# Cross-attention kernel: the query products moved ahead of the value products, and odd slots in a second PSUM bank until the first output

## The chip, the cores and the metric

The kernel runs on one core of a Trainium2 chip. The metric is the device time of one execution in microseconds. The core has a matrix engine (TensorE, PE in the profile), which writes to the eight banks of PSUM; a vector engine (VectorE, DVE), a scalar engine (ScalarE, ACT) and a general engine (GpSimd, POOL); and a sync engine (SyncE, SP) that issues nearly all transfers. The engines run their own instruction streams in program order and meet through semaphores.

## The reference

`x` is 4 x 2048 x 640, the context 4 x 77 x 1024; of its 77 tokens the last 4 are image tokens (`ip`). There are 20 heads of 32 channels.

```
q = heads(x @ W_q); k_t = heads(text @ W_k); v_t = heads(text @ W_v)
probs_t = softmax(q k_t^T * scale)
text_out = probs_t v_t
attn_scores = q k_ip^T * scale
qsem = l2norm(probs_t @ text)                    # per head, 1024 channels
sem = qsem @ l2norm(ip)^T
probs_ip = softmax(attn_scores + 0.5 * sem) * spatial_mask
ip_out = probs_ip v_ip
out = (text_out + ip_out) @ W_out + b_out + x
```

## The kernel before

A prologue of about 88 us works the context and the weights into tables: keys per group of four heads (`kbd`), and a value table `xm` that holds, for each head, the Gram matrix of the text tokens (for the length in `l2norm`), the products with the image tokens, a column of ones and the values. Numbers that need more than 16 bits or more than the fast 32-bit form go as two parts, hi and lo, so that most products are three matmuls (hi x hi, hi x lo, lo x hi).

The main loop runs over 16 tiles of 512 rows of `x`. A tile is five slots (one for each group of four heads, 128 columns of q), a slot is two pairs of 256 rows, and a pair is one step p of the loop; there are 160, ten to a tile. All five engines have a loop over p, written out by hand, and in each the order of the work inside a step is the order of the code. In step p, PE does:

- the scores of pair p (6 matmuls to `ps_S`, L1278). In even steps they wait for the slot's query (`q_lo`), in all for DVE and ACT to have read the last scores (`s_read`, `p_ready`);
- transposes of one piece of the next tile of `x` into `ps_M` (L1294), in steps 0, 1, 2, 7 and 8 of ten;
- from step 16 on a part of the output matmuls of the tile before, in the banks `ps_O` and `ps_O2` in turn (L1257), 11 to 17 of them, in all steps of ten;
- the value products U of pair p - 2 (16 matmuls to `ps_U`, L1354), which wait for the transposed probabilities (`pts_loaded`) and for DVE to have read the last U (`attn_ready`);
- half of the query products of a coming slot m (`ps_Q`, L1368): in odd steps, p = 2m - 3, the first 7 of 15 matmuls, in even steps the other 8. The first half waits for `q_lo >= m`, that is, until DVE has read slot m - 1 out of the bank. For the first slot of a tile each three matmuls wait for their piece of `x` (`xT_lo`); the fifth piece is transposed in the same even step in which its products stand.

In step p, DVE adds finished output to `x` (L1139), takes the maximum of the scores and their bias (L1153, L1160), in odd steps forms the lo part of the query (L1127, which signals `q_lo`), forms the lo part of a piece of `x` (L1127, `xT_lo`), and only then works on U of pair p - 2 (L1185 to L1224; in odd steps some ten small instructions more, to L1241). ACT copies the hi parts of query and `x` (L1001, L1007), takes the exponentials (L1038) and copies them as 16-bit numbers (L1050), POOL forms their lo parts (L1120), and SP issues their DMA transposes (L951), which U of that pair needs two steps later.

```
PASSES = ((0, 0), (0, 1), (1, 0))
Q_MMS = [(c, a, m) for c in range(CC) for a, m in PASSES]
Q_PARTS = (Q_MMS[:7], Q_MMS[7:])
XT_AT = {-10: 0, -9: 1, -8: 2, -3: 3, -2: 4}
OUT_FROM = min(OUT_AT)      # 6
```

Of the kernel before, what the change touches and what calls it, by code (L numbers as in the profile page):

```python
# [10 lines left out]
ACT = mybir.ActivationFunctionType  # L11
# [722 lines left out]
def main_loop(nc, top, g):  # L734

    P, B, S, C, T, T_ALL, CC = (g[k] for k in "P B S C T T_ALL CC".split())
# [3 lines left out]
    ps_S2, ps_U2, ps_Q, ps_M = (g[k] for k in "ps_S2 ps_U2 ps_Q ps_M".split())  # L740
    ident, wq, wo, mask_sb, inv_out, inv_eps, ip_unit = (
        g[k] for k in "ident wq wo mask_sb inv_out inv_eps ip_unit".split())
# [5 lines left out]
    STEPS = 2 * CC  # L748
    OUTS = 2 * SUB
    X_RING, XT_RING, AT_RING, P_RING, SIP_RING, PH_RING, PT_RING = NI, 8, 10, 3, 3, 2, 2  # L750
    VW_RING = IT_RING = 2
    LU = 2
    PASSES = ((0, 0), (0, 1), (1, 0))
# [3 lines left out]
    Q_MMS = [(c, a, m) for c in range(CC) for a, m in PASSES]  # L757
    Q_PARTS = (Q_MMS[:7], Q_MMS[7:])
# [18 lines left out]
    xT = [[sb(f"xT{r}_{k}", [P, TILE], F32R) for k in range(2)] for r in range(XT_RING)]  # L777
    qT = [[sb(f"qT{r}_{k}", [P, TILE], F32R) for k in range(2)] for r in range(2)]
# [28 lines left out]
    xT_ready, xT_hi, xT_lo = g["xT_ready"], sem("xT_hi_done"), sem("xT_lo_done")  # L807
    q_ready, q_hi, q_lo = sem("q_ready"), sem("q_hi_done"), sem("q_lo_done")
# [13 lines left out]
    o_bank = [g["ps_O"], g["ps_O2"]]  # L822
# [11 lines left out]
    OUT_FROM = min(OUT_AT)  # L834
# [9 lines left out]
    def pair_of(p):  # L844
        return p if 0 <= p < PAIRS else None
# [4 lines left out]
    def q_at(p):  # L850

        part = (p + 1) % 2
        m = slot_of(p + 3 - part)
        return None if m is None else (m, part)

    def x_at(p):
# [2 lines left out]
            return [(0, c) for c in range(CC)]  # L859
        return [(j, c) for at, c in XT_AT.items() for j in range(1, TILES) if STEPS * j + at == p]  # L860

    def x_bank(j, c):
        return ps_M if j else g["x_bank0"][c]

# [16 lines left out]
    with nc.Block() as block:  # L881
# [109 lines left out]
        @block.scalar  # L991
        def _(act):
            for p in range(FIRST, LAST):

                done = q_at(p - 1)
                if done is not None and done[1] == 1:
                    m = done[0]
                    act.wait_ge(q_ready, m + 1)
                    if m >= 2:
                        act.wait_ge(s_ready, 2 * (m - 1))  # L1000
                    nc.scalar.activation(qT[m % 2][0][:], ps_Q[:], ACT.Copy).then_inc(q_hi, 1)  # L1001
                for j, c in x_at(p):
                    act.wait_ge(xT_ready, CC * j + c + 1)
                    n = CC * j + c
                    if n >= XT_RING:
                        act.wait_ge(q_ready, CC * ((n - XT_RING) // CC + 1))
                    nc.scalar.activation(xT[n % XT_RING][0][:], x_bank(j, c)[:], ACT.Copy).then_inc(xT_hi, 1)  # L1007
                i = ip_at(p)
                if i is not None:
                    act.wait_ge(pip_ready, CC * (i + 1))  # L1010
                    if i >= 1:
                        act.wait_ge(*ring(ipT_loaded, i - 1))
                    else:
                        act.wait_ge(ones_set, 1)
                    for dst in (ip16[:, :, 0, 0:IPR], ip16[:, :, 1, IPR - IP_LO:2 * IPR - IP_LO]):
                        last = nc.scalar.activation(dst, pip[:], ACT.Copy)
                    last.then_inc(ip_hi, 1)
                m = slot_of(p - 6)
                if m is not None:

                    act.wait_ge(f_ready, m + 1)
                    nc.scalar.activation(f[:], f[:], ACT.Exp, scale=SCALE).then_inc(ef_ready, 1)
                m = slot_of(p - 4)
                if m is not None:

                    act.wait_ge(attn_ready, 2 * (m + 1))
                    if m >= 2:
                        act.wait_ge(*ring(aT_loaded, m - 2))
                    nc.scalar.activation(at16[m % 2][:, 0], attn[m % 2][:].rearrange("p s h d -> p s (h d)"),
                                         ACT.Copy).then_inc(at_hi, 1)  # L1030
                if pair_of(p) is not None:

                    act.wait_ge(bias_ready, p + 1)
                    if p >= P_RING:
                        act.wait_ge(n2_done, p - P_RING + 1)
                    for j in range(2):
                        for h in range(HG):
                            last = nc.scalar.activation(pr[p % P_RING][:, j, h, :], sc[:, j, h, 0:T], ACT.Exp,  # L1038
                                                        bias=bias[p % 2][:, j, h:h + 1], scale=SCALE)
                        last.then_inc(p_ready, 1)  # L1040

                    if p < PH_RING:
                        act.wait_ge(cleared, PH_RING)
                    for j in range(2):
                        act.wait_ge(p_ready, 2 * p + j + 1)
                        if p >= PH_RING:
                            act.wait_ge(*ring(pts_loaded[j], p - PH_RING))
                        hi = ph[p % PH_RING][:, j].rearrange("p h k c -> p h (k c)")
                        for col in (0, P + LO_B):
                            last = nc.scalar.activation(hi[:, :, col:col + T], pr[p % P_RING][:, j], ACT.Copy)  # L1050
                        last.then_inc(ph_ready, 1)
# [72 lines left out]
        def _(v):  # L1124
            def lo_part(dst, src, hi, hi_done, n, signal):
                v.wait_ge(hi_done, n)
                nc.vector.tensor_tensor(dst, src, hi.bitcast(F32), ALU.subtract).then_inc(signal, 1)  # L1127
# [5 lines left out]
            for p in range(FIRST, LAST):  # L1133
# [28 lines left out]
                done = q_at(p - 1)  # L1162
                if done is not None and done[1] == 1:
                    m = done[0]
                    lo_part(qT[m % 2][1][:], ps_Q[:], qT[m % 2][0][:], q_hi, m + 1, q_lo)
                for j, c in x_at(p):
                    one = xT[(CC * j + c) % XT_RING]
                    lo_part(one[1][:], x_bank(j, c)[:], one[0][:], xT_hi, CC * j + c + 1, xT_lo)
# [76 lines left out]
        def _(pe):  # L1245
# [16 lines left out]
            for p in range(FIRST, LAST):  # L1262
                if pair_of(p) is not None:
# [8 lines left out]
                    for j in range(2):  # L1272
# [4 lines left out]
                        for a, m in PASSES:  # L1277
                            last = nc.tensor.matmul(g["ps_S"][j][:, 0:GK], qT[slot % 2][a][:, q * P:(q + 1) * P],  # L1278
                                                    kbd[:, m, slot % CC, :], start=(a, m) == PASSES[0],
                                                    stop=(a, m) == PASSES[-1])  # L1280
# [17 lines left out]
                for i, half, piece in out_at(p):  # L1298

                    n = OUTS * i + half  # L1300
                    if piece == 0 and n >= 2:
                        pe.wait_ge(o_added, n - 1)
                    if half == 0:
                        for k in range(2 * piece, min(2 * piece + 2, CC)):
                            pe.wait_ge(*ring(aT_loaded, CC * i + k))
                    if half == 0 and piece == len(O_PIECES) - 1:
                        pe.wait_ge(*ring(ipT_loaded, i))
                        if i % NI == 0:
                            b = i // NI
                            pe.wait_ge(vw_loaded[b % VW_RING], 64 * (b // VW_RING + 1) + 16)  # L1310
                    last = output_matmuls(i, half, O_PIECES[piece], o_bank[half % 2])
                    if piece == len(O_PIECES) - 1:
                        last.then_inc(o_ready, 1)

                for half, part in END_AT.get(p - PAIRS, ()):

                    i = TILES - 1
# [17 lines left out]
                    last = output_matmuls(i, half, END_PARTS[part], end_bank[half])  # L1335
                    if part == 3:
                        last.then_inc(o_ready, 1)

                u = pair_of(p - LU)
                if u is not None:  # L1340

# [12 lines left out]
                                last = nc.tensor.matmul(uo[:, j, h, :], pts[u % PT_RING][0:n, j, 2 * h + tile, :],  # L1354
                                                        xm[0:n, tile, k0 * HG + h, :], start=tile == 0, stop=tile == 1)
                    last.then_inc(u_ready, 1)

                if q_at(p) is not None:

                    m, part = q_at(p)  # L1360
                    i, k = divmod(m, CC)
                    mms = Q_PARTS[part]
                    if part == 0 and m:
                        pe.wait_ge(q_lo, m)
                    for c, a, b_ in mms:
                        if k == 0 and (a, b_) == PASSES[0]:
                            pe.wait_ge(xT_lo, CC * i + c + 1)
                        last = nc.tensor.matmul(ps_Q[:], wq[a][:, c, k * P:(k + 1) * P], xT[(CC * i + c) % XT_RING][b_][:],  # L1368
                                                start=(c, a, b_) == Q_MMS[0], stop=(c, a, b_) == Q_MMS[-1])
                    if part == 1:  # L1370
                        last.then_inc(q_ready, 1)


# [21 lines left out]
```

## Time and profile before

| | |
|---|---|
| median of 3 runs | 1023.91 us (1021.89 to 1025.69) |
| profiled execution | 1022.47 us, its span 1020.6 us |
| PE, DVE, ACT, POOL busy | 95%, 80%, 68%, 64% |
| TensorE clock granted, mean | 0.988 |
| chain that ended last | PE 77%, DMA 5%, DVE 4%, ACT 2% |

The page is of one profiled execution. PE's matmuls are pipelined: a group's record overlaps the start of the next, so where one group begins and the next begins says what it costs, and where the record ends says when its result is there. The chain is followed back from the last instruction, and says where a saved microsecond would be one at the end of the kernel.

### The profile page before, as it was taken

What the parts mean: (1) busy time and instruction counts of PE and PEld (TensorE: products, weight loads), DVE (VectorE), ACT (ScalarE), POOL (GpSimd) and SP (SyncE); (2) the same over time, 40 slices, a digit from 0 to 9 for tenths busy, and PEclk for the clock granted to TensorE, in tenths of its full rate; (3) what the DMA queues carried; (4) which work ended last, traced back from release to release, by engine and by line L of the source; (5) the groups of instructions that cost most, each with busy time, mean ns of one, the idle gap of its engine ahead of it and who ended that gap; (6) DMA issues with size and microseconds to landing.
All of it is one profiled execution on the core that took longest, in us unless ns stands there. A gap on an engine that the chain in (4) does not pass through costs nothing.

```text
span 1020.6 us, 24929 instructions
## 1 busy us (share of the span) xinstructions
PE 969.2 (95%) x7684; PEld 803.6 (79%) x7684; DVE 816.6 (80%) x2409; ACT 695.6 (68%) x2332; POOL 655.2 (64%) x1906
## 2 busy tenths in 40 slices
PE   5987788999999999999999999999999999999988
PEld 5875666888878888888887888888878888888855
DVE  6685698888888887888888888878878888878872
ACT  3534887777776777767776777777667777777740
POOL 3224587776676667677766777676667767776761
PEclk9978999999999999999999999999999999999999
DMA  9936999989889998899899989998899989887973
GB/s 293 298 117 161 195 179 186 177 163 180 168 186 186 186 185 177 163 176 162 174 178 192 192 164 191 169 167 173 167 190 187 180 169 190 137 157 154 149 138 111
DMA packets 488147, 180.27 MB, mean 177 GB/s; under 512 B 449694, under 2 KB 467155, under 8 KB 488015
## 3 DMA queue, kind: packets, MB, share of 16 engines
q1 hardware_dynamic: 487983, 178.63, 86.3%
q8 instruction: 61, 1.00, 0.4%
q14 instruction: 71, 0.58, 0.2%
q10 hardware_dynamic: 32, 0.07, 0.0%
HBM read 42.34 MB, written 27.22 MB: 68 GB/s over the span
## 4 chain that ended last, share of the span: by engine, by line
PE 77%; DMA 5%; DVE 4%; ACT 2%; issue 2%; SPq 2%; POOL 1%; DVEq 0%; ACTq 0%; POOLq 0%
PE ps_O L1257 25%; PE ps_Q L1368 25%; PE ps_S L1278 12%; PE ps_U L1354 11%; DMA pts<-ph 4%; PE ps_M L1294 3%; ACT pr L1038 2%; DMA x_in<-in_x_dram 1%; SPq L951 1%; DVE pr L1199 0%; PE ps_U L1257 0%; DVE n L1211 0%; ACT ph L1050 0%; DVE bias L1160 0%; SPq L924 0%
## 5 line engine op out<-in xcount | busy, mean ns | idle before, releaser
L1038 ACT ACTIVATE pr<-ps_S,bias 128x73 f32<-128x73 f32 x1280 | 288.8, 339 | 101.3 <-DVE bias L1160 100.1
L1120 POOL TENSOR_TENSOR ph<-pr,ph 128x220 f16<-128x220 f32 (+1 forms) x640 | 274.0, 460 | 126.2 <-ACT ph L1050 126.2
L1368 PE MATMUL ps_Q<-xT,wq_hi 128*128 128x512 f32 x800 | 280.1, 415 | 5.2 <-DVE qT L1127 5.2
L1257 PE MATMUL ps_O<-wo_hi,aT 128*128 128x320 f16 x1220 | 279.2, 300 | 0.0
L1050 ACT ACTIVATE ph<-pr 128x292 f16<-128x292 f32 x640 | 241.2, 500 | 0.0
L1257 PE MATMUL ps_O<-wo_lo,aT 128*128 128x320 f16 x610 | 182.3, 299 | 0.0
L1354 PE MATMUL ps_U<-xm,pts 128*128 128x110 f16 (+1 forms) x2560 | 159.3, 212 | 14.9 <-DMA pts<-ph 13.5
L1368 PEld LDWEIGHTS ps_Q<-xT,wq_hi 128*128 128x128 f32 x800 | 146.2, 191 | 32.7 <-DVE qT L1127 6.5
L1354 PEld LDWEIGHTS ps_U<-xm,pts 128*128 128x128 f16 (+1 forms) x2560 | 144.4, 98 | 32.3 <-issue 11.8
L1278 PE MATMUL ps_S<-kbd,qT 128*128 128x308 f32 x960 | 163.0, 304 | 2.6 <-ACT pr L1038 2.1
L1278 PEld LDWEIGHTS ps_S<-kbd,qT 128*128 128x128 f32 x960 | 150.8, 188 | 18.6 <-issue 3.0
L1368 PE MATMUL ps_Q<-xT,wq_lo 128*128 128x512 f32 x400 | 159.5, 399 | 0.0
L1257 PEld LDWEIGHTS ps_O<-wo_hi,aT 128*128 128x128 f16 x1220 | 119.2, 98 | 47.8
L1153 DVE TENSOR_REDUCE smax<-ps_S 128x8 f32<-128x584 f32 x160 | 121.6, 760 | 36.3 <-PE ps_S L1278 36.0
L1211 DVE TENSOR_REDUCE n<-pr 128x8 f32<-128x584 f32 x160 | 120.8, 755 | 0.0
L1199 DVE TENSOR_TENSOR pr<-ps_U,pr 128x584 f32<-128x584 f32 x160 | 116.9, 731 | 0.1
L1185 DVE COPY nd<-ps_U 128x40 f32<-128x40 f32 x160 | 31.5, 197 | 103.0 <-PE ps_U L1354 101.8
L1077 POOL TENSOR_TENSOR yt<-y 128x16 f32<-128x16 f32 x240 | 51.5, 215 | 91.8 <-DVE y L1241 79.2
L1007 ACT ACTIVATE xT<-ps_M 128x512 fp32r<-128x512 f32 x76 | 45.8, 603 | 76.4 <-PE ps_M L1294 76.4
L1094 POOL TENSOR_TENSOR at<-attn,at 128x512 f16<-128x512 f32 x80 | 92.7, 1159 | 0.0
L1368 PEld LDWEIGHTS ps_Q<-xT,wq_lo 128*128 128x128 f32 x400 | 76.3, 191 | 14.6
L1257 PEld LDWEIGHTS ps_O<-wo_lo,aT 128*128 128x128 f16 x610 | 59.9, 98 | 18.5
(228 smaller groups left out, 1338.9 us busy)
## 6 DMA issues: line engine op xcount, KB each, us to landing
out_dram<-x_in SPq DMA_DIRECT2D x64, 320.0 KB, 2.6
x_in<-in_x_dram SPq DMA_DIRECT2D x56, 320.0 KB, 3.2
pts<-ph SPq DMA_TRANSPOSE x320, 3.4
w_k<-in_L_xattn_W_k_dram SPq DMA_DIRECT2D x5, 512.0 KB, 8.8
w_ip<-in_L_xattn_W_k_ip_dram SPq DMA_DIRECT2D x1, 2560.0 KB, 11.0
w_v<-in_L_xattn_W_v_dram SPq DMA_DIRECT2D x5, 512.0 KB, 8.3
w_ip<-in_L_xattn_W_v_ip_dram SPq DMA_DIRECT2D x1, 2560.0 KB, 10.6
x_in<-in_x_dram SPq DMA_DIRECT2D x2, 1280.0 KB, 7.2
```

The lines of the kernel that those rows point to most:

```text
L1038: last = nc.scalar.activation(pr[p % P_RING][:, j, h, :], sc[:, j, h, 0:T], ACT.Exp, bias=bias[p % 2][:, j, h:h + 1], scale=SCALE)
L1050: last = nc.scalar.activation(hi[:, :, col:col + T], pr[p % P_RING][:, j], ACT.Copy)
L1077: nc.gpsimd.tensor_tensor(yt[:], y[:], y[:], ALU.mult).then_inc(newton_step, 1)
L1094: nc.gpsimd.tensor_tensor(at16[m % 2][:, 1], attn[m % 2][:].rearrange("p s h d -> p s (h d)"), at16[m % 2][:, 0], ALU.subtract).then_inc(a ...
L1120: nc.gpsimd.tensor_tensor(lo, full[:, :, t0:t1], one[:, :, 0, t0:t1], ALU.subtract).then_inc(pl_ready, 1)
L1153: nc.vector.tensor_reduce(smax[p % 2][:], sc[:, :, :, 0:T], AX.X, ALU.max).then_inc(max_done, 1)
L1199: nc.vector.tensor_tensor(pr[u % P_RING][:], uo[:, :, :, 0:T], pr[u % P_RING][:], ALU.mult).then_inc(prod_done, 1)
L1211: nc.vector.tensor_reduce(n2[un % 2][:, subs], pr[u % P_RING][:], AX.X, ALU.add).then_inc(n2_done, 1)
L1257: last = nc.tensor.matmul(bank[:, 0:HALF], stationary, moving, start=(k, a, b_) == O_MMS[0], stop=(k, a, b_) == O_MMS[-1])
L1278: last = nc.tensor.matmul(g["ps_S"][j][:, 0:GK], qT[slot % 2][a][:, q * P:(q + 1) * P], kbd[:, m, slot % CC, :], start=(a, m) == PASSES[0] ...
L1354: last = nc.tensor.matmul(uo[:, j, h, :], pts[u % PT_RING][0:n, j, 2 * h + tile, :], xm[0:n, tile, k0 * HG + h, :], start=tile == 0, stop= ...
L1368: last = nc.tensor.matmul(ps_Q[:], wq[a][:, c, k * P:(k + 1) * P], xT[(CC * i + c) % XT_RING][b_][:], start=(c, a, b_) == Q_MMS[0], stop=( ...
```

## The change

In PE's step the query products stand ahead of the value products; they are the same matmuls. The query products of odd slots below 8 (`FREE_SLOTS = (6 + 10) // 2`) go to `ps_O` instead of `ps_Q`, and their readers on ACT and DVE read there. Their first half waits for the last slot that used the same bank: for slots 0 to 7 two slots back, and from slot 9 on the slot before, as in the kernel before. The first output matmul waits until slot 7 has been read.

```
+    FREE_SLOTS = (OUT_FROM + STEPS) // 2
+
+    def q_bank(m):
+        return o_bank[0] if m % 2 and m < FREE_SLOTS else ps_Q
+
+    def q_bank_before(m):
+        used = [n for n in range(max(m - 2, 0), m) if q_bank(n) is q_bank(m)]
+        return used[-1] if used else None
...
-                    nc.scalar.activation(qT[m % 2][0][:], ps_Q[:], ACT.Copy).then_inc(q_hi, 1)
+                    nc.scalar.activation(qT[m % 2][0][:], q_bank(m)[:], ACT.Copy).then_inc(q_hi, 1)
...
-                    lo_part(qT[m % 2][1][:], ps_Q[:], qT[m % 2][0][:], q_hi, m + 1, q_lo)
+                    lo_part(qT[m % 2][1][:], q_bank(m)[:], qT[m % 2][0][:], q_hi, m + 1, q_lo)
...
+                    if n == 0 and piece == 0:
+                        pe.wait_ge(q_lo, FREE_SLOTS)
...
+                if q_at(p) is not None:
+
+                    m, part = q_at(p)
+                    i, k = divmod(m, CC)
+                    mms = Q_PARTS[part]
+                    if part == 0 and q_bank_before(m) is not None:
+                        pe.wait_ge(q_lo, q_bank_before(m) + 1)
+                    for c, a, b_ in mms:
+                        if k == 0 and (a, b_) == PASSES[0]:
+                            pe.wait_ge(xT_lo, CC * i + c + 1)
+                        last = nc.tensor.matmul(q_bank(m)[:], wq[a][:, c, k * P:(k + 1) * P], xT[(CC * i + c) % XT_RING][b_][:],
+                                                start=(c, a, b_) == Q_MMS[0], stop=(c, a, b_) == Q_MMS[-1])
+                    if part == 1:
+                        last.then_inc(q_ready, 1)
+
                 u = pair_of(p - LU)
                 if u is not None:
...
-                if q_at(p) is not None:
-
-                    m, part = q_at(p)
-                    i, k = divmod(m, CC)
-                    mms = Q_PARTS[part]
-                    if part == 0 and m:
-                        pe.wait_ge(q_lo, m)
```

PE, the end of an odd step of the main loop and the start of the next, before:

```order
L1257 MATMUL ps_O<-vw,ipT 128x320 x2
L1354 MATMUL ps_U<-xm,pts 128x110 [waits pts_loaded0_1,attn_ready]
L1354 MATMUL ps_U<-xm,pts 128x110 x7
L1354 MATMUL ps_U<-xm,pts 128x110 [waits pts_loaded1_1]
L1354 MATMUL ps_U<-xm,pts 128x110 x7
L1368 MATMUL ps_Q<-xT_0,wq_hi 128x512 [waits q_lo_done]
L1368 MATMUL ps_Q<-xT_1,wq_hi 128x512
```

and now:

```order
L1267 MATMUL ps_O<-vw,ipT 128x320 x2
L1361 MATMUL ps_Q<-xT_0,wq_hi 128x512 [waits q_lo_done]
L1361 MATMUL ps_Q<-xT_1,wq_hi 128x512
L1361 MATMUL ps_Q<-xT_0,wq_lo 128x512
L1361 MATMUL ps_Q<-xT_0,wq_hi 128x512
L1361 MATMUL ps_Q<-xT_1,wq_hi 128x512
L1361 MATMUL ps_Q<-xT_0,wq_lo 128x512
L1361 MATMUL ps_Q<-xT_0,wq_hi 128x512
L1381 MATMUL ps_U<-xm,pts 128x110 [waits pts_loaded0_1,attn_ready]
L1381 MATMUL ps_U<-xm,pts 128x110 x7
```

The query products and their wait for the bank moved ahead of the value products; the next step's scores now follow the value products at once.

PE, the even step in which a new tile's first slot is finished (here of the second tile), from the last output matmuls on, before:

```order
L1257 MATMUL ps_O<-vw,ipT 128x320 x2
L1354 MATMUL ps_U<-xm,pts 128x110 [waits pts_loaded0_0,attn_ready]
L1354 MATMUL ps_U<-xm,pts 128x110 x7
L1354 MATMUL ps_U<-xm,pts 128x110 [waits pts_loaded1_0]
L1354 MATMUL ps_U<-xm,pts 128x110 x7
L1368 MATMUL ps_Q<-xT_1,wq_hi 128x512
L1368 MATMUL ps_Q<-xT_0,wq_lo 128x512
L1368 MATMUL ps_Q<-xT_0,wq_hi 128x512 [waits xT_lo_done]
L1368 MATMUL ps_Q<-xT_1,wq_hi 128x512
L1368 MATMUL ps_Q<-xT_0,wq_lo 128x512
L1368 MATMUL ps_Q<-xT_0,wq_hi 128x512 [waits xT_lo_done]
```

and now:

```order
L1267 MATMUL ps_O<-vw,ipT 128x320 x2
L1361 MATMUL ps_Q<-xT_1,wq_hi 128x512
L1361 MATMUL ps_Q<-xT_0,wq_lo 128x512
L1361 MATMUL ps_Q<-xT_0,wq_hi 128x512 [waits xT_lo_done]
L1361 MATMUL ps_Q<-xT_1,wq_hi 128x512
L1361 MATMUL ps_Q<-xT_0,wq_lo 128x512
L1361 MATMUL ps_Q<-xT_0,wq_hi 128x512 [waits xT_lo_done]
```

The wait for the fifth piece of `x` (the second of the two) no longer has the value products ahead of it.

## Rows read from the trace of the kernel before

**Rows 1.** The page's first part: busy us, share of the span, instructions.
```profile
PE 969.2 (95%) x7684; PEld 803.6 (79%) x7684; DVE 816.6 (80%) x2409; ACT 695.6 (68%) x2332; POOL 655.2 (64%) x1906
```
**Rows 2.** Busy by stretch: length, PE, PEld, DVE, ACT, POOL, PE clock, DMA share, GB/s.
```profile
60.00:90.00 30.00, 22.58 (x116) 18.67 (x117) 22.02 (x56) 13.68 (x23) 8.04 (x8) 0.79 0.26 73
...
150.00:200.00 50.00, 44.09 (x350) 36.55 (x349) 41.60 (x130) 38.65 (x135) 37.35 (x110) 1.00 0.98 182
...
400.00:500.00 100.00, 100.00 (x814) 83.87 (x813) 84.61 (x261) 74.60 (x259) 69.75 (x210) 1.00 0.89 170
```
**Rows 3.** Waits, whole span: waiting line, awaited line, us in total, times, longest.
```profile
DVE nd L1185 <- PE ps_U L1354: 101.8, 111, 2.1
...
PE ps_U L1354 <- DMA pts<-ph: 13.5, 24, 1.4
...
PE ps_Q L1368 <- DVE qT L1127: 5.2, 6, 1.4
```
**Rows 4.** Waits from 105 to 180 us.
```profile
PE ps_U L1354 <- DMA pts<-ph: 9.4, 18, 1.2
```
**Rows 5.** Timeline of PE, steps 58 and 59: start, length, instruction, idle before it.
```profile
414.66 0.98 PE L1354 MATMUL ps_U<-xm,pts 128*128 128x110 f16 x16
...
417.40 1.01 PE L1278 MATMUL ps_S<-kbd,qT 128*128 128x308 f32 x6
...
420.57 0.98 PE L1354 MATMUL ps_U<-xm,pts 128*128 128x110 f16 x16
...
421.37 0.70 PE L1368 MATMUL ps_Q<-xT,wq_hi 128*128 128x512 f32 x2
```
**Rows 6.** Timeline of DVE in the same steps.
```profile
416.02 0.19 DVE L1185 COPY nd<-ps_U 128x40 f32<-128x40 f32 x1
...
418.51 0.75 DVE L1153 TENSOR_REDUCE smax<-ps_S 128x8 f32<-128x584 f32 x1
...
419.51 0.68 DVE L1127 TENSOR_TENSOR qT<-ps_Q,qT 128x512 fp32r<-128x512 f32 x1
...
421.59 0.20 DVE L1185 COPY nd<-ps_U 128x40 f32<-128x40 f32 x1 [1.40 <-PE ps_U L1354]
```
**Rows 7.** Timeline, steps 66 and 67: DVE, and PE's scores of step 67.
```profile
460.33 0.20 DVE L1185 COPY nd<-ps_U 128x40 f32<-128x40 f32 x1 [0.21 <-PE ps_U L1354]
...
462.06 1.02 PE L1278 MATMUL ps_S<-kbd,qT 128*128 128x308 f32 x6
...
463.11 0.77 DVE L1153 TENSOR_REDUCE smax<-ps_S 128x8 f32<-128x584 f32 x1 [0.68 <-PE ps_S L1278]
...
464.11 0.68 DVE L1127 TENSOR_TENSOR qT<-ps_Q,qT 128x512 fp32r<-128x512 f32 x1
```
**Rows 8.** Timeline, U of step 67 and step 68: PE and DVE.
```profile
464.85 0.97 PE L1354 MATMUL ps_U<-xm,pts 128*128 128x110 f16 x16
...
465.86 0.20 DVE L1185 COPY nd<-ps_U 128x40 f32<-128x40 f32 x1 [0.47 <-PE ps_U L1354]
...
467.34 1.01 PE L1278 MATMUL ps_S<-kbd,qT 128*128 128x308 f32 x6
...
470.74 0.68 DVE L1127 TENSOR_TENSOR xT<-ps_M,xT 128x512 fp32r<-128x512 f32 x1
...
470.92 0.48 PE L1368 MATMUL ps_Q<-xT,wq_hi 128*128 128x512 f32 x1
...
472.17 0.63 PE L1368 MATMUL ps_Q<-xT,wq_hi 128*128 128x512 f32 x2
```
**Rows 9.** Timeline of ACT, step 68 and the start of step 69.
```profile
470.87 1.80 ACT L1038 ACTIVATE pr<-ps_S,bias 128x73 f32<-128x73 f32 x8 [0.78 <-DVE bias L1160]
...
473.86 0.64 ACT L1001 ACTIVATE qT<-ps_Q 128x512 fp32r<-128x512 f32 x1
```
**Rows 10.** Timeline of PE, the query products of slots 1 and 2.
```profile
97.33 0.73 PE L1368 MATMUL ps_Q<-xT,wq_hi 128*128 128x512 f32 x2 [1.41 <-DVE qT L1127]
...
105.53 0.73 PE L1368 MATMUL ps_Q<-xT,wq_hi 128*128 128x512 f32 x2 [1.42 <-DVE qT L1127]
```

More of the change, by code:

```diff
@@ L1356, in _ @@
                     last.then_inc(u_ready, 1)
-                if q_at(p) is not None:
-                    m, part = q_at(p)
-                    i, k = divmod(m, CC)
-                    mms = Q_PARTS[part]
-                    if part == 0 and m:
-                        pe.wait_ge(q_lo, m)
[L1365 to L1371, printed above, removed]
 _INS = ["x", "ctx_2048", "fside_S_0", "L0_xattn_W_q", "L0_xattn_W_k", "L0_xattn_W_v", "L0_xattn_W_k_ip",
```

## The prediction

> **What bounds the kernel now.** I read the page's first part, then busy time by stretches, then the list of waits, then the timeline of single steps. The reader should see first that PE is busy for 95% of the span [rows 1], and that this is not even: from 400 to 500 us it never stands idle, from 150 to 200 us it is idle for 5.9 of 50 us [rows 2]. So from the first output matmuls on (about 180 us) the end is set by PE's own work, and a microsecond that PE waits there is a microsecond of the run. Before that, the loop of scores, exponentials, transposes and value products is bound by its latency.
>
> In the list of waits, PE's largest in the main loop is for the transposed probabilities, 13.5 us in 24 pieces, of which 9.4 us lie between 105 and 180 us [rows 3, 4]. The wait for the query bank is 5.2 us. The row that decides this case is another one: DVE waits 101.8 us, in 111 of 160 steps, for the value products (ps_U) [rows 3]. It starts its work on a step's value products the moment that PE has finished them. A step that moves those products later moves DVE's work later.
>
> **What the change does, part by part.** Names: step p; Q1 and Q2 are the first 7 and last 8 matmuls of a slot's query products; Q1 stands in odd steps, Q2 in even ones. Nothing is added or removed, but one wait that is met long before; the same 7684 matmuls run. On PE a step was scores, transposes, output, U, Q, and becomes scores, transposes, output, Q, U.
>
> *The odd steps from 17 on.* Q1 must wait until DVE has read the previous slot out of ps_Q (q_lo). In step 59 the scores start at 417.40 and U at 420.57 [rows 5]; DVE's last read of ps_Q ends at 419.51 + 0.68 = 420.19 [rows 6]. It looks as if Q1 could stand at 420.57 without waiting. But DVE reaches that read by an unbroken run that starts with the copy of U's result of the step before, at 416.02: 420.19 - 416.02 = 4.17 us, with no idle in it [rows 6]. Before, Q2 stood between that U and the scores of step 59: 417.40 - 414.66 - 0.80 = 1.94 us of it [rows 5]. Now U comes last: its record (0.98 us) reaches 0.18 us beyond the next group's start (U 420.57, Q 421.37 [rows 5]), DVE picks up 0.04 us after the end (421.55 to 421.59 [rows 5, 6]), and I take 0.05 us for the way back. So Q1 may start 0.18 + 0.04 + 4.17 + 0.05 = 4.44 us after the scores' start, and PE is there after 420.57 - 417.40 = 3.17 us: a wait of 1.27 us. Step 67 has fewer output matmuls and no output addition on DVE: 464.79 - 460.33 less 0.68 us idle = 3.78 us against 464.85 - 462.06 = 2.79 us [rows 7, 8], so 0.18 + 0.04 + 3.78 + 0.05 - 2.79 = 1.26 us. A tile has five odd steps, three like 59 and two like 67: 6.3 us.
>
> Queued behind the waiting Q1 on PE are U, then the next step's scores; DVE waits for U, so the delay goes once round the loop and nothing takes it back. DVE can't use the time, since its next work is what it waits for.
>
> *The even steps before a new tile (p = 10j - 2).* Q2 there ends with three matmuls on the fifth piece of the new tile, which DVE finishes in the same step. Step 68: from the copy of U's result (465.86) to the end of that piece (470.74 + 0.68 = 471.42) is 5.56 us [rows 8], the heavier of DVE's two kinds of step. Now the piece is there 0.18 + 0.04 + 5.56 + 0.05 = 5.83 us after the scores' start. PE wants it after 470.92 - 0.80 - 467.34 = 2.78 us (to U's place, since its 0.80 us no longer precede) plus 472.17 - 470.92 = 1.25 us for five matmuls, 4.03 us [rows 8]. The wait is 1.8 us, once a tile.
>
> *The exponentials.* The scores of an odd step now come right after U, and overwrite what ACT still reads: in step 68 the exponentials start 470.87 - 465.82 = 5.05 us after the odd step's U ended and last 1.80 us [rows 8, 9]. The scores will be held back by up to a microsecond, but this lies inside the wait of Q1, which comes later. ACT's copy of the query product ends at 474.50, 8.7 us after that U [rows 9]; with DVE's 0.68 us behind it this is a little later than the 4.44 us above in the pair with the fewest output matmuls. I take 0.3 us a tile, between 0 and 0.5.
>
> Sum of a tile: 6.3 + 1.8 + 0.3 = 8.4 us. Steps 17 to 156 hold 14 tiles: +118 us. Against this, PE's waits for transposes after 180 us, 13.5 - 9.4 = 4.1 us, now fall behind Q, with some small ones: -5 us.
>
> *The first sixteen steps.* Two of the bank's waits go at once, 1.41 and 1.42 us [rows 10], since slots 0 to 7 alternate banks. In the rest PE's idle is mostly for the transposes, and Q now fills it. What follows late is DVE and ACT, each needing its turn before the next scores, and DMA, whose share is 0.98 there [rows 2]: most of the fill will come back as another wait. At best all of the 9.4 us and the 2.8 us go (-12); step 15, already in one bank and with no output matmuls as cover, costs about 3 us more. I take -4, range -12 to +3.
>
> Sum: the profiled execution took 1022.5 us (span 1020.6), 1.4 us under the median of the runs, 1023.9. 1022.5 + 118 - 5 - 4 = 1131 us, +10.7%.
>
> The Trainium skill ("Perfetto Trace Analysis", Matmuls) says that independent groups should rotate through PSUM banks so that the reading of one overlaps the matmuls of the next. No run here shows it yet. By that rule alone only the slots that now rotate would change, 2.8 us less and 1020 us in all, since from slot 9 on the bank is shared as before; the sum goes by DVE's run in rows 6 instead.
>
> **The rivals.**
> 1. *The query wait is met.* If DVE's read stays where it is, 0.38 us before the place of Q1 (420.19 against 420.57), the waits for transposes go and nothing comes: 1022.5 - 13.5 = 1009 us. For it: the rows of that step, read alone. It decides if q_lo still comes within 3.17 us of the scores' start. Against: 101.8 us in which DVE waits for U itself. Chance 6%.
> 2. *Only the odd steps wait.* If the tile's fifth piece is not late, or its wait comes off the next one: 1022.5 + 14 x 6.3 - 9 = 1102 us. Chance 9%.
> 3. *The slower side.* The held-back scores are not covered and cost PE some 0.5 us a pair as well: 70 x 0.5 = 35 us, 1166 us. For it: ACT's 1.80 us of exponentials start only when DVE is through [rows 9]. Chance 5%.
> 4. *The clock.* From 60 to 90 us PE was busy for 22.6 of 30 us and its granted clock was 0.79; from 150 to 200 us it was busy for 44.1 of 50 us at 1.00 [rows 2]. In the new kernel the same 969 us of work [rows 1] would stand in 1131 us, 86%, near the second stretch's 88%. If it were granted 0.79 after all, the 780 us or so from the first output matmuls to the last query products would need 780 x (1/0.79 - 1) = 207 us more: about 1338 us. Chance 1%. The Trainium skill ("TensorE: Matmul & The Clock Gate", A second HAM failure mode) tells of a kernel whose short idles between groups made the clock go up and down; the stretch from 150 to 200 us speaks against it here.
> 5. *DVE catches up* and the change nets nothing, 1020 to 1028 us: 3%.
>
> **How the numbers follow.** The forecast, both waits in the sizes worked out, has 76%: 1131, on its own from 1115 to 1148 (8.4 us a tile by one more or less, and the bounds of the start). For 8 in 10 the range takes in part of rivals 2 and 3: 1100 to 1150. Half a per cent is what a measurement of this kernel can tell. Faster: rival 1, 6%. Same: 3%. Slower: 91%.
>
> **What would show it.** Right: PE's wait for the query bank (DVE qT) about 70 times at 1.2 to 1.3 us, some 90 us in all, ending DVE's wait for U as before; 14 waits for an xT piece of about 1.8 us; PE's waits for transposes below 5 us; each tile 8.4 us longer between the same two rows; PE's busy share near 86%. The first scores come 1.4 us earlier. Wrong: if the query waits are under 0.5 us, DVE's run after U was not what set them; if the scores wait for ACT and Q1 does not wait, the bound is rival 3's; if the time is under 1095 us, the step that fails is that U's delay reaches q_lo in full.

## The result, and the profile after

The changed kernel takes 1140.16 us (median of 4 runs, 1137.87 to 1142.8) beside 1024.61 us of the kernel before in the same session: a ratio of 1.1137, 95% interval 1.1111 to 1.1163. The prediction was 1131 us, 1100 to 1150. The profiled execution took 1137.87 us with a span of 1136.1 us. The same 7684 matmuls run as in [rows 1], and PE is busy for 89% of a longer span. Its busy time rose from 969.2 to 1013.6 us all the same, which is waiting too for the most part (see the end of this section):

```profile
PE 1013.6 (89%) x7684; PEld 783.4 (69%) x7684; DVE 821.6 (72%) x2409; ACT 697.8 (61%) x2332; POOL 655.5 (58%) x1906
```

The stretches that answer to [rows 2] (length, PE, PEld, DVE, ACT, POOL, PE clock, DMA share, GB/s) show where PE stands. From 400 to 500 us it was busy for all 100 us; now it is busy for 92.87, and it starts 713 matmuls in place of 814. Its granted clock stays at 1.00 there.

```profile
60.00:90.00 30.00, 22.72 (x121) 18.24 (x122) 23.05 (x58) 14.95 (x25) 9.39 (x9) 0.85 0.29 82
150.00:200.00 50.00, 41.75 (x301) 32.51 (x299) 37.05 (x115) 35.92 (x125) 33.88 (x105) 0.93 0.92 167
400.00:500.00 100.00, 92.87 (x713) 70.82 (x711) 73.91 (x224) 66.13 (x228) 61.55 (x185) 1.00 0.75 148
```

The list of waits, for [rows 3], has three waits of PE that are new or have grown (the query bank's was 5.2 us, the one for `pr` 2.1 us, and there was none for an `xT` piece), while the one for the transposed probabilities is down from 13.5 to 4.3 us. DVE's wait for the value products has more than doubled.

```profile
DVE nd L1195 <- PE ps_U L1381: 243.7, 128, 4.9
...
PE ps_S L1288 <- ACT pr L1048: 33.0, 50, 2.3
PE ps_Q L1361 <- DVE qT L1137: 28.4, 44, 1.9
...
PE ps_Q L1361 <- DVE xT L1137: 17.9, 14, 1.5
```

The chain of work that ended last changes from nearly all PE (PE 77%, DVE 4% before) to a loop of two engines:

```profile
PE 45%; DVE 33%; issue 7%; ACT 6%; DMA 1%; POOL 0%; DVEq 0%; SPq 0%
```

The loop can be read in steps 60 and 61, the pair behind 58 and 59 of [rows 5, 6], with fewer output matmuls. First PE, then DVE:

```profile
467.20 0.99 PE L1381 MATMUL ps_U<-xm,pts 128*128 128x110 f16 x16
468.56 1.45 PE L1288 MATMUL ps_S<-kbd,qT 128*128 128x308 f32 x6 [0.37 <-ACT pr L1048]
...
472.27 0.73 PE L1361 MATMUL ps_Q<-xT,wq_hi 128*128 128x512 f32 x2 [0.33 <-DVE qT L1137]
...
474.01 0.98 PE L1381 MATMUL ps_U<-xm,pts 128*128 128x110 f16 x16
```
```profile
468.23 0.20 DVE L1195 COPY nd<-ps_U 128x40 f32<-128x40 f32 x1
...
471.04 0.58 DVE L1170 TENSOR_SCALAR bias<-smax 128x8 f32<-128x8 f32 x1
471.54 0.68 DVE L1137 TENSOR_TENSOR qT<-ps_Q,qT 128x512 fp32r<-128x512 f32 x1
...
475.03 0.20 DVE L1195 COPY nd<-ps_U 128x40 f32<-128x40 f32 x1 [2.22 <-PE ps_U L1381]
```

U of step 60 ends at 468.19. DVE starts 0.04 us later, runs 3.99 us without a gap to the end of the lower query part (472.22), and Q1 starts 0.05 us after that. U then ends at 474.99, and DVE, idle for 2.22 us, starts at 475.03. The scores in between wait too: they could stand at 467.20 + 0.80 = 468.00 and start at 468.56, and their own 1.45 us (1.01 in [rows 5]) hold a wait for the second half's exponentials. PE thus spends only 0.33 us of the loop's slack at Q1 and the rest at the scores; the place of Q1 is the same either way.

From the scores of step 17 to those of step 157 the time went from 784.5 to 898.2 us, +113.7; the start of step 17 came 2.7 us later and the part behind step 157 is 1.0 us shorter. The sum, 115.4 us, is the difference of the two spans. In the loop PE's idle time went from 5.7 to 76.2 us and its busy time from 778.8 to 822.0, with the same matmuls at a mean granted clock of 1.00: a wait inside a group's record, as in the scores of step 61, or one that its end covers, counts as busy.

### The profile page after: what moved, and what is told of

The parts are those of the page before. It is cut to its first block, busy times and chain, and to the rows that moved or that the text cites. A ratio compares the mean times of both kernels' runs of the same rounds, so it can differ in the third digit from the quotient of the medians.

```text
span 1136.1 us, 24929 instructions
## 1 busy us (share of the span) xinstructions
PE 1013.6 (89%) x7684; PEld 783.4 (69%) x7684; DVE 821.6 (72%) x2409; ACT 697.8 (61%) x2332; POOL 655.5 (58%) x1906
## 4 chain that ended last, share of the span: by engine, by line
PE 45%; DVE 33%; issue 7%; ACT 6%; DMA 1%; POOL 0%; DVEq 0%; SPq 0%
PE ps_Q L1361 18%; PE ps_O L1267 11%; PE ps_U L1381 9%; DVE smax L1163 6%; DVE pr L1209 5%; ACT pr L1048 5%; PE ps_S L1288 4%; DVE n L1221 3%; DVE attn L1234 3%; DVE qT L1137 2%; DVE bias L1170 2%; DVE w_sem L1204 2%; DVE x_in L1149 2%; PE ps_M L1304 1%; DVE f L1241 1%
## 5 line engine op out<-in xcount | busy, mean ns | idle before, releaser
L1361 PE MATMUL ps_Q<-xT,wq_hi 128*128 128x512 f32 x760 | 269.7, 420 | 46.2 <-DVE qT L1137 28.4
L1288 PE MATMUL ps_S<-kbd,qT 128*128 128x308 f32 x960 | 194.2, 326 | 41.5 <-ACT pr L1048 33.0
L1361 PEld LDWEIGHTS ps_Q<-xT,wq_hi 128*128 128x128 f32 x760 | 137.6, 190 | 100.2 <-DVE qT L1137 50.2
L1288 PEld LDWEIGHTS ps_S<-kbd,qT 128*128 128x128 f32 x960 | 141.1, 190 | 67.9 <-issue 41.4
L1381 PEld LDWEIGHTS ps_U<-xm,pts 128*128 128x128 f16 (+1 forms) x2560 | 133.9, 99 | 49.4 <-issue 45.5
L1361 PE MATMUL ps_Q<-xT,wq_lo 128*128 128x512 f32 x380 | 151.0, 397 | 0.0
L1032 ACT ACTIVATE f<-f 128x64 f32<-128x64 f32 x80 | 20.6, 257 | 166.0 <-DVE f L1241 166.0
L1361 PEld LDWEIGHTS ps_Q<-xT,wq_lo 128*128 128x128 f32 x380 | 72.2, 190 | 13.8
```

The source lines that it names most:

```text
L1361: last = nc.tensor.matmul(q_bank(m)[:], wq[a][:, c, k * P:(k + 1) * P], xT[(CC * i + c) % XT_RING][b_][:], start=(c, a, b_) == Q_MMS[0], s ...
```

## The experiments

Each ratio is to the kernel before in the same session, whose median was 1021.4 to 1024.6 us. Three measures are used below. *Loop*: the time from the scores of step 17 to those of step 157. *Late at the scores, late at Q*: the sum, over these 140 steps, of what the spacing of matmul starts exceeds the same spacing in the kernel before, for scores and for query products. In the changed kernel the two come to 119.5 us; waits for transposes that went, and other small ones, take off the 5.8 us by which the loop's growth is less. *Closing*: the time from the end of DVE's lower query part to the next Q1, median by kind of odd step. The median is over the runs; the last four columns are of one profiled execution each.

| kernel | median us | ratio to before | loop us | late at scores | late at Q | closing us |
|---|---|---|---|---|---|---|
| before | 1024.61 | | 784.5 | 0 | 0 | 0.84 to 1.32 |
| changed | 1140.16 | 1.1137 | 898.2 | 67.8 | 51.7 | 0.05 |
| order_only | 1159.69 | 1.1349 | 897.5 | 67.0 | 51.6 | 0.06 |
| banks_only | 1022.91 | 1.0009 | 784.1 | 0 | -1.3 | 0.83 to 1.32 |
| odd_only | 1088.79 | 1.0664 | 846.3 | 52.8 | 11.6 | 0.06 (0.25 in one kind) |
| even_only | 1081.16 | 1.0580 | 838.9 | 5.4 | 53.3 | 0.06 |
| half_norm | 1116.40 | 1.0911 | 875.7 | 49.6 | 47.3 | 0.05 |
| exp_pairs | 1127.22 | 1.1028 | 888.6 | 14.6 | 95.3 | 0.05 |
| x_late | 1110.11 | 1.0859 | 867.9 | 67.4 | 21.5 | 0.05 |
| head_only | 1024.83 | 1.0019 | 782.2 | 0 | -1.3 | 0.82 to 1.32 |
| even_at_late | 1063.63 | 1.0391 | 820.6 | 11.3 | 28.9 | 0.05 (0.25 in one kind) |
| even_qlo_first | 1060.48 | 1.0367 | 819.2 | 23.0 | 12.3 | 0.05 |
| odd_exp_pairs | 1073.98 | 1.0519 | 833.4 | 7.7 | 35.7 | 0.05 |
| before_exp_pairs | 1017.79 | 0.9956 | 781.8 | 0 | -0.6 | 0.06 to 1.35 |

The last column is the result in short: wherever query products stand ahead of the value products in odd or in even steps, Q1 starts 0.05 or 0.06 us after DVE has let the bank go (0.25 in one kind of step of two kernels). In the kernel before it came about a microsecond later, and DVE's run could be that much longer at nearly no cost. before_exp_pairs has such a case: in the first kind of odd step the run is 5.34 us in place of 4.35, its closing falls from 0.96 to 0.06 us, and Q1 starts only 0.09 us later after the scores.

**Parts of the change: bank or order.** In all variants of the order the block of the query products stands in both places, ahead of the value products and behind them, and a condition chooses:

```
-    FREE_SLOTS = (OUT_FROM + STEPS) // 2
+    FREE_SLOTS = 0                       # order_only alone
...
+                q_first = True           # order_only; False in banks_only
-                if q_at(p) is not None:
+                if q_first and q_at(p) is not None:
...
+                if not q_first and q_at(p) is not None:
```

> The order of before (query products behind the value products), and odd slots below 8 in the second bank: the part of the change on the banks alone. Theory: of the waits for the query bank before the first output, 5.2 us in 6 pieces, most turn into other waits, since DVE and ACT must be through before the next scores anyway; 1019 us, that is 0 to 5 us less than before. Rival (all of them are gained): 1017 us. Rival (the bank is nothing): 1022 to 1024 us.

> Query products ahead of the value products in all steps, one bank throughout. Theory: the steady part costs what it costs in the changed kernel (tiles of 64.1 us), and the first eight slots now wait for the bank too, with nothing ahead of them: 1140 + 3 to 15, about 1147 us. Rival (the second bank gave nothing): 1140 us.

banks_only: 1.0009, interval 0.9996 to 1.0022. In the old order the second bank brings nothing in the total, which is the second rival. order_only: 1.1349, interval 1.1329 to 1.1370, and 1160 us where 1147 was expected. Its loop is that of the full change to 0.7 us; what lies ahead differs, since the scores of step 17 start at 204.8 us against 184.6 with the bank. So the order makes all of the loss, and the bank repairs some 20 us that the order costs at the start. From 105 to 180 us order_only shows waits that the bank removes (PE's list of waits):

```profile
PE ps_Q L1362 <- DVE qT L1137: 11.8, 6, 3.6
```

They are a part of it only. From the first scores to those of step 17 order_only takes 105.9 us and the changed kernel 89.5; PE is idle for 24.0 and 16.1 us of these, and busy for 81.9 and 73.3, at a mean granted clock of 0.82 and 0.94. So about half of the difference stands as busy time, beside 37.5 us at the lower of the two clock levels (1.2 GHz) in place of 10.2. The expectation had counted waits alone.

**Odd and even steps.** `q_first = p % 2 == 1` and `q_first = p % 2 == 0`.

> Query products ahead of the value products in odd steps only (first halves, Q1); in even steps behind them as before; second bank as in the changed kernel. The prediction's wording, that the cost comes because the second half (Q2) no longer stands between the even step's U and the next scores, would give no wait at all here: about 1015 to 1022 us. The loop account (DVE works on both steps' U in series: from the end of an odd step's U to the lo part of the query in the next odd step 9.2 to 9.8 us, then Q1 1.74 us and U 1.0 us, a loop of about 12.0 us where PE's own work is 11.1) gives waits of 0.4 to 1.3 us in odd steps and 1.0 us once a tile for the fifth piece of x, 5.4 us a tile: about 1093 us. Rival (each of the two moves costs half): 1081 us.

> Query products ahead of the value products in even steps only (second halves, Q2); first halves behind U as before; second bank as in the changed kernel. Loop account: DVE's read comes 4.44 us after the scores' start as in the changed kernel's sum, but Q1 now has U's 0.80 us as cover again, so the wait is about 0.47 us in each odd step (0.6 in one of five); the fifth piece of x comes 1.74 us earlier than in the changed kernel and costs 0.1 us: 2.5 us a tile, about 1052 us. The prediction's wording gives nearly the full cost of the odd steps less 0.8 us each: the same 1052. Rival (each move costs half): 1081 us.

The two losses are 61.8 and 54.4 us of loop, 116.2 together, and the full change has 113.7: they add. odd_only came out near its sum (1088.8 us, 1093 expected), but PE hardly waits at Q1 there:

```profile
PE ps_S L1288 <- ACT pr L1048: 14.3, 42, 2.3
...
PE ps_Q L1362 <- DVE qT L1137: 2.4, 2, 2.0
```

Its DVE shows why. After U of the odd step (its heavy kind of work) it runs on into the next step's work without a gap, from 448.34 to 457.59; Q1 starts at 457.65, and the copy of the next U follows at 460.40. That is a loop of 12.06 us for a pair: DVE's work for two steps (9.25), 0.06 to Q1, then Q1 and U (2.75), where the kernel before needs 11.1.

```profile
448.34 0.20 DVE L1195 COPY nd<-ps_U 128x40 f32<-128x40 f32 x1 [2.82 <-PE ps_U L1382]
...
453.83 0.19 DVE L1195 COPY nd<-ps_U 128x40 f32<-128x40 f32 x1
...
456.90 0.69 DVE L1137 TENSOR_TENSOR qT<-ps_Q,qT 128x512 fp32r<-128x512 f32 x1
...
460.40 0.20 DVE L1195 COPY nd<-ps_U 128x40 f32<-128x40 f32 x1 [2.21 <-PE ps_U L1382]
```

even_only missed its sum by 29 us, and its 1081.2 us is the figure of the rival by which each move costs half. That rival names no mechanism, and odd_only is 8 us off it. The loop was the expected one (closing 0.06 us), but DVE's run in it was 4.43 us in four of five kinds of odd step. The experiment on GpSimd below is about that.

**Is DVE's run the loop's length?** Half of the text norm is left out in half_norm, whose VectorE sum then goes over 37 of 73 columns:

```
-  nc.vector.tensor_reduce(n2[un % 2][:, subs], pr[u % P_RING][:], AX.X, ALU.add).then_inc(n2_done, 1)
+  nc.vector.tensor_reduce(n2[un % 2][:, subs], pr[u % P_RING][:, :, :, 0:37], AX.X, ALU.add).then_inc(n2_done, 1)
```

> The changed kernel, but VectorE's norm sum of each pair (L1221, 0.75 us) adds only 37 of the 73 columns, so half of the text norm is left out. If the loop U of the even step, VectorE's run, lower query part, next query bank sets the odd steps, the run gets some 0.38 us shorter, the five odd steps of a tile 1.9 us, and the wait for the fifth x piece up to 0.4: tiles of 61.9 us instead of 64.1 and about 1108 us in all (1104 to 1114). If ScalarE's exponentials or the scores' wait for them hold the step instead (rival), the time stays at 1137 to 1143.

1116.4 us, 8 us above the figure, 2 above its range and far from the rival's. The instruction fell by less than assumed, from 760 to 460 ns, and what it fell by shows in the time. DVE's runs of the first four kinds of odd step are 0.31 to 0.34 us shorter, that of the fifth is not (its bias is stretched, see below), and the wait for the fifth x piece falls by 0.31 us: 1.6 us in sum, and a tile takes 62.54 us in place of 64.11, 1.57 less.

**Are the held-back scores a cost of their own?** In exp_pairs the exponentials of two heads go in one instruction:

```
-  for h in range(HG):
-      last = nc.scalar.activation(pr[p % P_RING][:, j, h, :], sc[:, j, h, 0:T], ACT.Exp,
-                                  bias=bias[p % 2][:, j, h:h + 1], scale=SCALE)
+  for h in range(0, HG, 2):
+      last = nc.scalar.activation(pr[p % P_RING][:, j, h:h + 2, :], sc[:, j, h:h + 2, 0:T], ACT.Exp,
+                                  scale=SCALE * 0.01)
```

> The changed kernel, but ScalarE's exponentials take two heads at once with a fixed bias and a small scale, four instructions for a pair in place of eight, so the softmax maxima are left out and the probabilities are not those of the reference. This makes some 1 us less of ScalarE work a step. In the steady part PE stands 31.0 us at the scores for ScalarE and 44.4 us at the query products. If the waits at the scores are only the loop's own slack taken earlier, they go to the query bank's wait and the total falls by no more than 10 us, to 1130 to 1140. If they are a cost of their own (rival), up to 31 us go and the time is 1109 to 1115.

> The kernel with query products first in odd steps alone (measured 1089 us), and ScalarE's exponentials two heads at once with no bias and a small scale, so the softmax maxima are left out and the probabilities are not those of the reference; 1 us less of ScalarE work a step. In that kernel the scores start or run late by 52.8 us in all and the query products by 11.6 us. If a second loop (value products of the odd step, VectorE's run of the even step, exponentials, next scores) is the bound there, most of the 52.8 us go and Q's wait does not take their place, since Q2 stands ahead of the odd step's scores: 1040 to 1055 us. If the scores' delay only stands for the query bank's wait as in the full change (rival), no more than 10 us go: 1078 us or more.

> The control: the kernel before with the same shortened exponentials (softmax maxima left out). PE is without idle in most of the steady part there, so ScalarE's time should be worth nothing: 1017 to 1024 us, the first sixteen steps perhaps a few us shorter. If it falls by more, part of what the shortened exponentials bring in the other kernels has nothing to do with the change.

exp_pairs takes 1127.2 us, between its two ranges and nearer to the first. The lateness at the scores fell from 67.8 to 14.6 us, and that at Q rose from 51.7 to 95.3. PE's list of waits for exp_pairs, against the three rows of the changed kernel above:

```profile
PE ps_Q L1361 <- DVE qT L1137: 70.3, 71, 1.7
PE ps_Q L1361 <- DVE xT L1137: 17.6, 14, 1.5
...
PE ps_S L1288 <- ACT pr L1048: 4.4, 4, 1.4
```

Only 9.6 us of loop went. They are in DVE's run: by kind of odd step it is 3.68, 4.10, 4.24, 3.57 and 4.42 us, in the changed kernel 4.00, 4.14, 4.04, 4.04 and 4.42; the sum is 0.63 us less, and a tile is 0.61 us shorter. The scores' wait was the loop's slack spent earlier, as the prediction says. The control gained too, 0.9956 (0.9939 to 0.9973), so some 4 of the 13 us in the total need not have to do with the change. odd_exp_pairs fits neither expectation: I had taken the scores for the bound and forecast 1040 to 1055, and 1074 us came. The lateness went from 52.8 to 7.7 us at the scores and rose from 11.6 to 35.7 at Q, with a closing of 0.05 us in all kinds of odd step, and DVE's time for the five pairs of a tile is 45.5 us in place of 46.2: the bound is DVE's work for the pair, followed by Q1 and U. The separate loop through the exponentials that I proposed falls.

**The wait for the fifth x piece.** `q_first = p % 10 != 8`.

> The changed kernel, but in the one step of a tile that waits for the fifth x piece (steps 8, 18, 28 and so on) the query products stay behind the value products, as before the change. By the trace of the changed kernel that wait is 1.4 us in each of 14 tiles, and one of 2.7 us in step 8: some 20 us less, 1120 us (1115 to 1125). If the wait only moves to the next step's query bank, since that slot's copies then start later (rival), the time stays at 1135 to 1142.

1110.1 us, 30 us less than the full change, a larger gain than either theory gave. PE's wait for that piece falls from 17.9 us to that of the first row, and with U again ahead of Q2, DVE's work of step 9 of the tile starts earlier by Q2's length, so Q1 there comes 3.40 us after the scores in place of 4.70 in the changed kernel:

```profile
PE ps_Q L1396 <- DVE xT L1137: 5.2, 14, 0.6
...
PE ps_Q L1362 <- DVE qT L1137: 10.6, 30, 1.9
```

A tile takes 61.95 us, 2.16 less. The expectation had priced the 1.4 us of the wait and left out the odd step behind it.

**The start.** `q_first = p < 15`, with the banks of the change.

> The new order in steps 0 to 14 alone, with the second bank for odd slots below 8 as in the change; from step 15 the old order. The steady part should take its 784 us of before. If the new order does gain a little in the head (the prediction's 4 us), the time is 1016 to 1019 us beside 1021 to 1024 of before. By the trace of the changed kernel, where the head lost 4 to 7 us, of which some 3.6 in step 15 and 2.6 in step 8, it is 1021 to 1028.

1024.8 us, ratio 1.0019, interval 0.9997 to 1.0042: the new order gains nothing there. In the profiled executions the stretch from 95 to 185 us reads as follows, first the kernel before, then the changed one, banks_only and head_only:

```profile
95.00:185.00 90.00, 74.02 (x553) 60.00 (x553) 70.56 (x205) 70.09 (x243) 58.32 (x173) 1.00 0.97 182
```
```profile
95.00:185.00 90.00, 73.87 (x518) 58.12 (x517) 66.94 (x196) 65.71 (x232) 54.97 (x163) 0.94 0.96 181
```
```profile
95.00:185.00 90.00, 76.48 (x522) 62.41 (x521) 67.59 (x197) 65.17 (x228) 54.07 (x160) 0.91 0.94 177
```
```profile
95.00:185.00 90.00, 75.19 (x521) 59.92 (x520) 66.34 (x197) 65.45 (x229) 54.22 (x161) 0.92 0.92 173
```

PE starts 31 to 35 fewer matmuls in 90 us in all three, at a mean granted clock of 0.91 to 0.94 in place of 1.00. In the changed kernel the lower of the two levels (1.2 GHz) was granted from about 139 to 143 and from 173 to 180 us, behind and beside its two longest waits there, 2.67 us for the fifth piece (Q2 goes on at 138.23) and 1.87 us at the bank (Q1 at 174.15). banks_only has the old order, a clock as low and no longer total, so the order isn't shown to be the cause. Most of the changed kernel's longer start does stand beside the lower clock: from the first scores to those of step 17 it takes 6.6 us more than the kernel before (89.5 and 82.8), of which 5.1 us are PE's busy time (73.3 and 68.3) and 1.5 us its idle time (16.1 and 14.6). Inside the 10.2 us at the lower level its matmul starts are some 4 us further apart in sum than usual, an estimate from the spacing of each kind at the higher level. Why the level fell in one execution and not in the other stays open: before_exp_pairs, with the order and bank of before, has 3.4 us of it there too, from 139.5 us on.

**GpSimd beside VectorE.** In even_only PE waits 42.3 us for the query bank. The odd step whose scores start at 486.58 us, DVE then POOL:

```profile
489.49 0.18 DVE L1166 COPY s_ip<-ps_S 128x32 f32<-128x32 f32 x1
489.61 1.02 DVE L1170 TENSOR_SCALAR bias<-smax 128x8 f32<-128x8 f32 x1
490.55 0.68 DVE L1137 TENSOR_TENSOR qT<-ps_Q,qT 128x512 fp32r<-128x512 f32 x1
```
```profile
489.45 1.16 POOL L1104 TENSOR_TENSOR at<-attn,at 128x512 f16<-128x512 f32 x1
```

The bias handles 8 numbers a partition and takes as little as 0.17 us elsewhere. Here it takes 1.02 us and ends at 490.63, when POOL's instruction ends (490.61). The same holds in the rest of this trace: 59 of the 62 biases that take over 0.5 us end within 0.03 us of the end of a POOL instruction, 56 of them with this one. even_at_late moves that one instruction to the end of POOL's step; even_qlo_first lets DVE take the lower query part ahead of the bias:

```
-                    pool.wait_ge(at_hi, m + 1)          # even_at_late: ahead of the lo parts of ph
-                    nc.gpsimd.tensor_tensor(at16[m % 2][:, 1], attn[m % 2][:].rearrange("p s h d -> p s (h d)"),
-                                            at16[m % 2][:, 0], ALU.subtract).then_inc(at_lo, 1)
...
+                    pool.wait_ge(at_hi, m + 1)          # the same two, last in the step
+                    nc.gpsimd.tensor_tensor(at16[m % 2][:, 1], attn[m % 2][:].rearrange("p s h d -> p s (h d)"),
+                                            at16[m % 2][:, 0], ALU.subtract).then_inc(at_lo, 1)
```

> The kernel with query products first in even steps alone (measured 1081 us), and GpSimd's lower part of the attention result (at<-attn,at, 1.16 us, L1104) moved from the middle of its step to the end. In the trace of that kernel VectorE's bias, 0.17 us in most even steps, takes up to 1.07 us in odd steps while this GpSimd instruction runs and ends with it (490.63 and 490.61 us). If that overlap makes the query bank's wait, the bias falls to 0.2 to 0.3 us, the lower query part is ready 0.3 to 0.8 us earlier in 70 odd steps, and the time falls to 1035 to 1060 us. If the wait has another cause, or the stretch moves with GpSimd's work to another VectorE instruction of the same run (rival), the time stays at 1076 to 1084.

> The kernel with query products first in even steps alone (measured 1081 us), and VectorE takes the lower query part ahead of the bias instead of behind it. If PE's wait for the query bank (42.3 us, 71 times, in that kernel) follows the end of VectorE's run, each of 70 waits shortens by the bias before it, 0.17 to 1.0 us, mean near 0.55: time 1040 to 1060 us. The exponentials then start 0.6 us later after the scores; if they take over as the bound (rival), the time is 1075 us or more.

even_at_late: 1063.6 us, 17.5 less, 4 above its range and far from the rival's 1076. The bias takes over 0.5 us in 2 steps in place of 62 and 35.9 us in all in place of 69.8. Part of the gain is given back at the fifth x piece, 13.1 us of wait. even_qlo_first: 1060.5 us, just above its range; its runs to the lower query part are 3.47 to 3.93 us, and the scores, whose exponentials now start later, are late by 23.0 us.

No variant that keeps the arithmetic beats the kernel before; its loop holds 5.7 us of PE idle in 784.5, and no variant's loop is more than 3 us shorter (head_only 782.2, before_exp_pairs, which leaves out the maxima, 781.8; one profiled execution each).

## Why the prediction was right, and where it was not

- *The bound.* That a microsecond of PE's waiting is one of the run held: the loop's +113.7 us and the total's +115.6 us agree but for 2 us.
- *The odd steps* (forecast 6.3 us a tile, with 0.3 for the exponentials). The loop is the one described: U's end to DVE 0.04 us, DVE's run, 0.05 us to Q1, in all five kinds of odd step. The run was taken as 4.17 and 3.78 us and is 4.00 to 4.42, over the five odd steps 20.64 us in place of 20.07. That is nearly all by which the rest of the tile is off: without the x piece (1.41 us), a tile grew by 8.65 - 1.41 = 7.2 us against 6.6.
- *Where the wait shows.* This wording failed: about 70 waits of 1.2 to 1.3 us at the query bank, some 90 us in all, were forecast, and there are 44 of 28.4 us, with 33.0 us at the scores in 50. The prediction had said that the scores are held back inside that wait; it did not follow that the wait named in the list shrinks by as much. Its own sign of failure, query waits under 0.5 us, would have misled in step 61 (0.33 us). The time to read is from one release to the next start, not the idle before one instruction.
- *The fifth x piece* (forecast 1.8 us). 1.41 us a tile: the sixth matmul of Q2, the first on that piece, starts 1.64 us after its neighbour in place of 0.23. The missing 0.4 us is DVE's small f<-nd,w_sem, which took 25.1 us in 80 instructions before and takes 14.5 us now: DVE's run was read from step 68 of the kernel before, where it was stretched, and now it meets POOL's work elsewhere (w_sem went from 19.8 to 37.5 us). The two misses, 0.6 us too little and 0.4 too much, nearly cancel in the tile, 8.65 us against 8.4; that it came so close is luck.
- *Waits for transposes.* Forecast below 5 us, measured 4.3, all before 182 us. For the loop 5 us less were forecast; 14 tiles of 8.65 us are 121.1, and the loop grew by 113.7, since 5.7 us of PE's idle and one stretch of 3.4 us at the lower clock (from 753.2 us) stand in the loop of the kernel before alone.
- *The start* (forecast -4 us) is the mis-sized term: the first scores come 3.9 us earlier (1.4 forecast), but step 17 starts 2.7 us later in place of 4 earlier, which is most of the 7 us by which 115.6 exceeds the forecast 109. The first scores lie at 95.2 to 97.8 us in the eleven kernels with the second bank and at 99.0 to 99.8 in the three without, so a part of the 3.9 us is the spread between executions. Two waits of [rows 10] went, but the scores of step 8 came 37.5 us after those of step 0 (36.5 before), step 8 waited 2.7 us for the second tile's fifth piece, which the prediction counted from step 18 on only, and step 15 waited 1.9 us at the bank. The sum had looked at waits alone; 5.1 of the 6.6 us by which this part grew are busy time, some 4 of them beside the lower granted clock, for which it had no term. banks_only and head_only show that neither bank nor order gains there.
- *The rivals.* The met wait (1009 us) and the catching up (1020 to 1028) are out by the total; the odd steps alone (1102) by the 14 waits for xT. The clock (1338) is out by 1.00 from 400 to 500 us. PE's share came to 89%, not 86, since its busy time came to 1013.6 us in place of the 969 taken. The slower side (1166) is out by the total and by exp_pairs. By the rule of the Trainium skill on rotating banks that the prediction cites ("Perfetto Trace Analysis", Matmuls) 2.8 us were to be gained. In banks_only PE's wait for the query bank in the first steps does fall, from 5.2 to 0.9 us, but the total measures 1.0009. Its waits for transposes stay (9.0 us, 9.4 before) and its granted clock from 95 to 185 us is 0.91; what took up the gain isn't shown.

## What to carry to other kernels

Ask of an order written out by hand what the next engine is waiting for: work that releases the engine whose answer you need next goes first, and work that needs that answer goes last, as far as this kernel shows. Here U released DVE and Q1 needed DVE, and the 1.94 us of Q2 between U and the next scores were the cover. Price such an edit by the loop from release to release over whole steps, since the wait will show wherever PE first meets it; and when a filler moves, look at the whole pair of steps, as both halves of this change cost by themselves and their costs added.

## What the runs showed of the hardware

A small VectorE instruction whose operands lie in SBUF can take six times as long beside a GpSimd instruction. The bias (128x8) is at 171 ns at least and at 1072 ns at most in even_only, ends (in 56 of the 62 cases over 0.5 us) within 0.03 us of the end of the GpSimd instruction `at<-attn,at`, and the profile shows this as length, not as idle. Over 160 steps it summed to 41.3 us before, 44.2 after, 69.8 in even_only and 35.9 once the GpSimd instruction was moved. The Trainium skill ("SBUF — State Buffer", Who interferes with whom) says that the two engines share a port pair that one instruction holds to its end, and that VectorE's tensor_scalar and its operations with two SBUF inputs can need it. The trace agrees in so far as the ends fall together, at 490.63 and 490.61 us in the step shown; the port itself shows in no row. So DVE's run depends on what GpSimd happens to do beside it: for one and the same work it was 3.62 us in even_at_late and 4.43 us in even_only, a difference of 0.8 us in a step of 6.
